# A four-layer recurrent model on one core: two products of each feed-forward row made ahead, in the score banks of the causal attention

## The chip, the core and the metric

The kernel runs on one core of one Trainium2 chip. The metric is the device time of the whole program in microseconds (us), as the median of several executions. PE is TensorE, DVE is VectorE, ACT is ScalarE, POOL is GpSimd and SP the engine that here only issues DMAs.

## The reference, cut to what matters

The model has a state of 2 x 1024 tokens of 128 channels. Each of four layers normalises the state, runs an attention over it and a feed-forward part, and adds their product to the state. All numbers are fp32. The change touches layers 2 and 3, whose attention is causal (16 heads of 8 channels); layer 2 turns queries and keys by rotary angles first, layer 3 has biases. Their feed-forward parts read the same normalised state x:

```
layer 2, 8 pairs of routed experts and one pair of shared ones, j = 0..8:
    y += W2[j] . ( gate(e, token) * silu(W1[j] . x) * (W3[j] . x) )      (no gate for j = 8)
layer 3, 16 experts, j = 0..15:
    a = min(Wg[j] . x + bg[j], 7),  b = clip(Wu[j] . x + bu[j], -7, 7)
    y += Wd[j] . ( gate(j, token) * a * sigmoid(1.702 a) * (b + 1) )
```

The gates come from a router: logits of x, a choice of experts by token, and weights that are zero for those not chosen. So every expert is computed for every token.

## The kernel before

`layer` (L3087) runs a layer: `attention_weights` and `ffn_weights` give tiles and pairs for their loads, then `rotary_attention` or `biased_attention` runs a prologue (normalise, queries, keys, values, split in bf16 parts that go through DRAM into "stacks"), then `causal_attention` (L2092), `project_out` (L2713) and the experts (`grouped_ffn`, L1185, in layer 2, `clamped_ffn`, L1289, in layer 3).

**The causal attention** has 8 units (two batches by four groups of four heads). Each unit needs two passes. The first finds the maximum of each row of scores: 20 "max" jobs on PE (L2393 to L2400) into one of two double banks (`room`), each reduced by one DVE instruction (L2276). After the 6th job (query half 0) and after the 20th (half 1) the maxima are negated and split in three bf16 parts on DVE, turned by one small matmul ("maxima", L2405), copied (L2301) and sent by two small DMAs into three more rows of the query stack (L2346). The second pass makes the scores again, transposed and with the maximum subtracted by those rows ("st", L2424, one of three score banks `st`), takes the exponential on ACT (L2365) and multiplies by the values ("pv", L2443). Steps of half 0 wait for the first maxima rows, those of half 1 for the second ones. When a half is done its context is copied by ACT (L2372), turned ("context", L2412) and divided on DVE.

The order of all this on PE, and with it on DVE, ACT and SP, is written by `work_order` (L2134), a small planner that runs when the program is built. It keeps a clock `now` of PE, a list of first-pass jobs and a list of second-pass events, each in its own order, estimates from fixed costs when the head of each list could start, and takes the earlier one. PE executes the result in order: a step that waits holds all behind it. SP's list of DMAs follows the same order, after the loads of the stacks of units 1 and 2 and of the feed-forward weights (L2336 to L2340). The last three jobs belong to the router (logits, and turning the gates), whose chain of small DVE instructions lies between them.

**The feed-forward parts** go over four chunks of 512 tokens and, in each, over the experts j; a pair (chunk, j) is a step, 36 in layer 2 and 64 in layer 3. PE makes two products of 128 x 128 by 128 x 512 per step (`up`) into banks `a` and `b`, three of each, two steps ahead, and then the step's third product into `y` (L1227, L1333). In layer 2 ACT takes silu of `a` (L1240), DVE multiplies it by `b` (`mid`, L1259) and by the gate (`hid`, L1264). In layer 3 ACT makes `below` from `a` (L1343) one step ahead of `acted` from `below` (L1357), so ACT's queue is below(n+1), acted(n); DVE makes `linear` from `b` (L1369), then `mid` (L1374) and `hid` (L1380). The gate of a step comes as a row spread over all partitions by DMA (`GateRows`, four tiles, a row is loaded when the tile's last reader is done).

Of the kernel before, what the change touches and what calls it, by code (L numbers as in the profile page):

```python
# [1034 lines left out]

class GateRows:
# [23 lines left out]
class GroupRouter(TailRouter):  # L1060
# [6 lines left out]
    def __init__(self, nc, k, ph, landed, tiles):  # L1067
        super().__init__(nc, k, ph, landed)
        self.wr, *self.wide = tiles
        E, G = self.E, 4  # L1070
# [57 lines left out]
class SoftmaxRouter(TailRouter):  # L1128
# [7 lines left out]
    def __init__(self, nc, k, ph, landed, tiles):  # L1136
# [4 lines left out]
        self.gate_room, self.up_bias = ph.sb("r_gate_room", [P, E]), ph.sb("r_up_bias", [P, E])  # L1141

    def pool(self, pool):

        self.nc.gpsimd.memset(self.top[:], self.SLOPE * self.LIMIT).then_inc(self.filled, 1)

# [7 lines left out]
    def vector(self, dve, n, src, job_free, count):  # L1154
# [3 lines left out]
        if n == self.LOGITS:  # L1158
# [3 lines left out]
            nc.vector.tensor_scalar(self.gate_room[:], self.bias[:, 0, :], -1.0, self.LIMIT, ALU.mult, ALU.add).then_inc(self.steps, 1)  # L1162
            nc.vector.tensor_scalar(self.up_bias[:], self.bias[:, 1, :], 1.0, None, ALU.add).then_inc(self.steps, 1)
            chain.n = 2
            dve.wait_ge(self.steps, 2)
# [14 lines left out]
def grouped_weights(nc, ph, w):  # L1180
    gate, wide = ph.sb("gate", [P, 16]), [ph.sb("wide_" + name, [P, w["w_" + name].shape[1], P]) for name in ("gate", "up", "down")]
    return (gate, *wide), [(gate[:], w["gate"])] + [(tile[:], w["w_" + name]) for tile, name in zip(wide, ("gate", "up", "down"))]


def grouped_ffn(nc, k, w, tiles, r):  # L1185
# [3 lines left out]
    N, M, AHEAD = NCH * J, J - 1, 2  # L1189
    with phase(nc, "f2") as ph:  # L1190
# [5 lines left out]
        with nc.Block() as block:  # L1196

            @block.sync
            def _(sp):
                for m in range(NCH * M):  # L1200
                    c, j = divmod(m, M)
                    c0, j0 = divmod(m - rows.KEPT, M)
                    srcs = [r.dram[e:e + 1, c * CHUNK:(c + 1) * CHUNK] for e in (2 * j, 2 * j + 1)]
                    rows.load(sp, m, srcs, hid_ready, c0 * J + j0 + 1)

            @block.tensor
            def _(pe):
                def up(n):
                    c, j = divmod(n, J)
                    x = k.xnT[:, c * CHUNK:(c + 1) * CHUNK]  # L1210
                    if n >= 3:
                        pe.wait_ge(act_ready, n - 2)
                    nc.tensor.matmul(a[n % 3][:], w1T[:, j, :], x, start=True, stop=True).then_inc(a_done, 1)
                    if n >= 3:
                        pe.wait_ge(mid_ready, n - 2)
                    nc.tensor.matmul(b[n % 3][:], w3T[:, j, :], x, start=True, stop=True).then_inc(b_done, 1)

                for n in range(AHEAD):
                    up(n)
                for n in range(N):  # L1220
                    c, j = divmod(n, J)
# [160 lines left out]

H = 16
# [1784 lines left out]
```

## Time and profile before

| | us |
|---|---|
| median of 3 runs (lowest, highest) | 1840.69 (1837.62, 1852.1) |
| the profiled execution, its own time | 1835.92 |
| its span in the trace | 1834.1 |
| PE busy, share of the span | 1523.2, 83% |
| DVE busy | 1168.7, 64% |
| ACT busy | 914.5, 50% |
| POOL busy | 473.3, 26% |
| layer 2: first matmul of the attention to last product of the experts | 932.0 to 1308 |
| layer 3: the same | 1351.4 to 1822.5 |

A busy time is the sum of an engine's instructions. Matmuls are pipelined, so a busy PE need not be at its peak. The granted clock (PEclk) is the mean share of TensorE's full clock of 2.4 GHz; it has two levels, 1.00 and 0.50 (1.2 GHz). In a timeline a bracket behind a group holds the idle time of its engine before it and what ended it.

### The profile page before, as it was taken

Reading aid. Unit: us, or ns where it says so; the run is one execution under the profiler, and the core shown is the slowest. Engines: PE = TensorE matmul, PEld = TensorE weight load, DVE = VectorE, ACT = ScalarE, POOL = GpSimd, SP = SyncE. Lnnn points to the kernel's source line nnn. Section 1 sums busy time; section 2 is a strip of 40 time slices with the busy share of each in tenths; the row PEclk is TensorE's granted clock in tenths of the full one; section 3 lists DMA queues with packets and bytes.
Section 4 is the critical chain, followed back from the end, with each engine's and each line's share of the span. In section 5 each row is a group of like instructions: output and inputs, shape, how many; then the busy total and the mean of one; then the engine's idle time right before and its main releaser. Section 6 shows DMA issues by size and latency. Waiting matters only on the chain. (4 is left out here: it accounts for less than half of the span.)

```text
span 1834.1 us, 32772 instructions
## 1 busy us (share of the span) xinstructions
PE 1523.2 (83%) x12067; PEld 733.9 (40%) x12067; DVE 1168.7 (64%) x2509; ACT 914.5 (50%) x1755; POOL 473.3 (26%) x408
## 2 busy tenths in 40 slices
PE   5989744998888888988748988889848988889998
PEld 4656422434433433334313434344323343344443
DVE  4323667745855855834668988635658988617777
ACT  1332232666656666665225666642224666555453
POOL 0701437756756756730210000000020000000000
PEclk9989865999999999999768999899868999789999
DMA  7232257666766666730240100022170010004332
GB/s 216 84 94 73 58 164 185 181 160 172 179 160 164 178 169 168 183 84 1 75 148 20 37 20 20 2 73 90 33 225 20 20 37 20 2 6 111 100 98 80
DMA packets 218198, 179.13 MB, mean 98 GB/s; under 512 B 57600, under 2 KB 186136, under 8 KB 217624
## 3 DMA queue, kind: packets, MB, share of 16 engines
q1 hardware_dynamic: 207928, 160.34, 32.4%
q10 hardware_dynamic: 8064, 12.51, 2.4%
q0 software_dynamic: 2048, 4.20, 0.8%
q8 instruction: 96, 1.57, 0.4%
q14 instruction: 62, 0.51, 0.1%
HBM read 108.64 MB, written 67.64 MB: 96 GB/s over the span
## 5 line engine op out<-in xcount | busy, mean ns | idle before, releaser
L1924 DVE TENSOR_REDUCE a1a_partial<-a1a_room 128x4 f32<-128x1024 f32 x192 | 226.4, 1221 | 30.8 <-PE a1a_room L1989 30.2
L2365 ACT ACTIVATE a3a_probsT<-a3a_st 128x512 f32<-128x512 f32 (+2 forms) x320 | 155.7, 560 | 123.5 <-PE a3a_st L2431 73.6
L1883 ACT ACTIVATE a1a_probsT<-a1a_st 128x512 f32<-128x512 f32 (+1 forms) x416 | 204.7, 575 | 13.9 <-PE a1a_st L2022 12.6
L2365 ACT ACTIVATE a2a_probsT<-a2a_st 128x512 f32<-128x512 f32 (+2 forms) x320 | 155.6, 560 | 111.1 <-PE a2a_st L2431 65.8
L2276 DVE TENSOR_REDUCE a3a_maxima<-a3a_room 128x2 f32<-128x1024 f32 (+3 forms) x160 | 170.2, 1113 | 34.5 <-PE a3a_room L2400 23.7
L2276 DVE TENSOR_REDUCE a2a_maxima<-a2a_room 128x2 f32<-128x1024 f32 (+3 forms) x160 | 170.2, 1113 | 25.6 <-PE a2a_room L2400 19.2
L1788 POOL TENSOR_TENSOR a1a_shifted<-a1a_shifted,a1a_best 128x1024 f32<-128x1024 f32 x64 | 121.7, 1903 | 93.5 <-DVE a1a_best L1930 67.2
L1920 DVE CUSTOM_DVE_ANT_0 a1a_shifted<-a1a_room,a1a_bands 128x256 f32<-128x256 f32 x256 | 93.3, 421 | 75.4 <-PE a1a_room L1989 67.4
L2059 PE MATMUL a1a_ctx<-a1a_probsT,a1a_vpad 128*9 128x512 f32 (+3 forms) x1408 | 139.3, 494 | 0.8
L1989 PE MATMUL a1a_room<-stack 48*128 48x128 bf16 (+1 forms) x1376 | 108.2, 261 | 37.1 <-DVE a1a_partial L1924 19.0
L2022 PE MATMUL a1a_st<-stack 51*128 51x512 bf16 (+3 forms) x576 | 116.7, 317 | 19.7 <-ACT a1a_nearT L1890 6.2
L1886 ACT ACTIVATE a1a_probsT<-a1a_st 128x512 f32<-128x512 f32 x128 | 73.3, 603 | 111.9 <-PE a1a_st L2031 111.9
L2325 POOL COPY a_vpad<-a_values 128x256 f32<-128x256 f32 x16 | 6.3, 400 | 423.9 <-PE a3a_ctx L2443 210.9
L2424 PE MATMUL a3a_st<-stack 51*128 51x512 bf16 (+3 forms) x384 | 87.5, 353 | 16.5 <-ACT a3a_probsT L2365 8.2
L2443 PE MATMUL a3a_ctx<-a3a_probsT,a_vpad 128*32 128x512 f32 (+3 forms) x768 | 90.0, 547 | 7.8 <-ACT a3a_probsT L2365 4.7
L2424 PE MATMUL a2a_st<-stack 51*128 51x512 bf16 (+3 forms) x384 | 84.7, 342 | 13.1 <-ACT a2a_probsT L2365 9.1
L1989 PEld LDWEIGHTS a1a_room<-stack 48*128 48x128 bf16 x1376 | 46.4, 99 | 117.7 <-DVE a1a_partial L1924 62.1
L2443 PE MATMUL a2a_ctx<-a2a_probsT,a_vpad 128*32 128x512 f32 (+3 forms) x768 | 86.4, 526 | 4.6 <-ACT a2a_ctxT L2372 2.0
L2393 PE MATMUL a2a_room<-stack 48*128 48x512 bf16 (+3 forms) x384 | 67.0, 351 | 25.5 <-PEq L2511 15.9
L1343 ACT ACTIVATE f_below<-f_a,r_r_gate_room 128x512 f32<-128x512 f32 x64 | 44.0, 687 | 85.7 <-PE f_a L1317 85.6
L2393 PE MATMUL a3a_room<-stack 48*128 48x512 bf16 (+3 forms) x384 | 66.9, 350 | 23.6 <-DMA stack<-k 14.0
L1800 POOL TENSOR_TENSOR a1a_beyond<-a1a_probsT,c_beyond_mask 128x512 f32<-128x512 f32 x56 | 70.9, 1271 | 55.1 <-ACT a1a_probsT L1886 55.1
(464 smaller groups left out, 3092.1 us busy)
## 6 DMA issues: line engine op xcount, KB each, us to landing
a1a_bands<-a_band SPq DMA_DIRECT2D x112, 192.0 KB, 3.8
a_near<-a1a_shifted SPq DMA_DIRECT2D x112, 192.0 KB, 3.1
a1a_near<-a_near SPq DMA_DIRECT2D x64, 256.0 KB, 4.0
f_rows<-l_gates SPq DMA_DIRECT2D x64, 256.0 KB, 3.0
a_band<-a1a_r_mix SPq DMA_DIRECT2D x64, 254.0 KB, 3.5
stack<-q SPq DMA_DIRECT2D x96, 96.0 KB
f_rows<-l_gates SPq DMA_DIRECT2D x64, 128.0 KB, 3.0
stack<-k SPq DMA_DIRECT2D x32, 96.0 KB
```

Of the source, the lines that this page charges most:

```text
L1788: nc.gpsimd.tensor_tensor(shifted[:, V % 2, t], shifted[:, V % 2, t], best[:, V % 2, :, t:t + 1].broadcast_to([P, HG, NEAR]), ALU.subtract ...
L1883: nc.scalar.activation(dst, src, ACT.Exp).then_inc(exp_done, 1)
L1920: ins = nc.vector.tensor_tensor_reduce(shifted[:, V % 2, t, place, :], src[:, place // 2, place % 2, :], band[i][:, place, :], 1.0, LOWEST ...
L1924: nc.vector.tensor_reduce(partial[:, g % 2, :, 1 + r].rearrange("p (a s) -> p a s", a=2), src, X_AXIS, ALU.max).then_inc(job_free, 1)
L1989: mm = nc.tensor.matmul(dst[:, lo + i * P:lo + (i + count) * P], q, rows_of(sides[edge], place, STACK)[:, c * P:(c + count) * P], start=Tr ...
L2022: mm = nc.tensor.matmul(dst[:, to:to + count * P], rows_of(sides[edge], place + j, ALL_ROWS)[:, c * P:(c + 1) * P], query_rows(q_stack, pl ...
L2059: mm = nc.tensor.matmul(ctx[32 * h:32 * h + DH + 1, lo * P:hi * P], vpad[b][right][:, c, h, :], probsT[:, block_index(V, at) % BLOCK_ROOMS ...
L2276: nc.vector.tensor_reduce(best, scores, X_AXIS, ALU.max).then_inc(job_free, 1)
L2365: nc.scalar.activation(probsT[:, block_at % BLOCK_ROOMS, place:place + heads, lo:], src, ACT.Exp).then_inc(exp_done, 1)
L2393: mm = nc.tensor.matmul(dst[:, end - width:end], query_rows(q_stack, place, STACK, I // HALF_TILES)[:, I % HALF_TILES * P:(I % HALF_TILES ...
L2424: mm = nc.tensor.matmul(dst[:, j * width:(j + 1) * width], rows_of(k_stack, place + j, ALL_ROWS)[:, c * P:(c + 1) * P], query_rows(q_stack ...
L2443: mm = nc.tensor.matmul(ctx[32 * PAIRED[h]:32 * PAIRED[h] + 32, lo:], vpad[b][:, c, PAIRED[h], :], probsT[:, block_at % BLOCK_ROOMS, h, lo ...
```

## The change

Of every chunk, the products of experts 0 and 1 (four products, 16 per layer) are made by PE inside `causal_attention`, as events "first" ahead of all second-pass events. Each goes through a score bank; ACT copies it to an SBUF tile (in layer 3 `below` and the biased `b` are made at once). Six of the 16 tiles lie in tensors that are idle then (two in `gT`, four in `xn_one`), ten are new. The planner takes a first product when its estimate is earlier than that of the next max job, from 4.0 us on. In the feed-forward part, the steps of experts 0 and 1 are moved between the others (`steps_of_chunks`), `up` skips them, and ACT and DVE read the tiles. The weights of these experts are loaded first, before the stacks of units 1 and 2; the rest is loaded where all was. In layer 3 the two bias tiles are made by POOL at the start instead of by DVE in the router's chain, and POOL's part of the router comes after unit 1's values instead of unit 3's.

```diff
+class FirstProducts:
+    EACH, TILES = 2, 10
+    COUNT = 2 * NCH * EACH
+    def __init__(self, nc, k, ph, landed, left, right):
+        self.nc, self.k, self.landed, self.weights = nc, k, landed, (left, right)
+        own, free = ph.sb("first", [P, self.TILES, CHUNK]), k.xn_one[:].rearrange("p t d -> p (t d)")
+        self.tiles = [k.gT[:, (NCH - 1 - i) * CHUNK:(NCH - i) * CHUNK] for i in range(2)]
+        self.tiles += [free[:, i * CHUNK:(i + 1) * CHUNK] for i in range(4)] + [own[:, i, :] for i in range(self.TILES)]
+    def place(self, c, j, side):
+        return self.tiles[(c * self.EACH + j) * 2 + side]
+    def tensor(self, pe, i, dst):
+        step, side = divmod(i, 2)
+        c, j = divmod(step, self.EACH)
+        if i == 0:
+            pe.wait_ge(*self.landed)
+        return self.nc.tensor.matmul(dst[:], self.weights[side][:, j, :], self.k.xnT[:, c * CHUNK:(c + 1) * CHUNK], start=True, stop=True)
+    def scalar(self, act, i, src):
+        return self.nc.scalar.copy(self.tiles[i], src[:])
+class ClampedProducts(FirstProducts):
...
+        if side == 0:
+            return self.nc.scalar.activation(self.tiles[i], src[:], ACT.Relu, bias=self.room[:, j:j + 1], scale=-1.0)
+        return self.nc.scalar.activation(self.tiles[i], src[:], ACT.Identity, bias=self.bias[:, j:j + 1])
+def steps_of_chunks(J, places):
+    later = [j for j in range(FirstProducts.EACH, J)]
+    for j, at in enumerate(places):
+        later.insert(at, j)
+    return [(c, j) for c in range(NCH) for j in later]
...
 def grouped_ffn(nc, k, w, tiles, r):
+    N, AHEAD, first = NCH * J, 2, r.first
+    seq = steps_of_chunks(J, (2, 6))
+    made = [n for n in range(N) if seq[n][1] >= first.EACH]
...
+                issued = 0
                 for n in range(N):
-                    if n + AHEAD < N:
-                        up(n + AHEAD)
+                    while issued < min(len(made), sum(m <= n for m in made) + AHEAD):
+                        up(issued)
+                        issued += 1
...
+                    if j < first.EACH:
+                        src = first.place(c, j, 0)
+                    else:
+                        q = made.index(n)
+                        act.wait_ge(a_done, q + 1)
+                        src = a[q % 3][:]
+                    nc.scalar.activation(acted[:, n % 3, :], src, ACT.Silu).then_inc(act_ready, 1)
...
 def clamped_ffn(nc, k, w, tiles, r):
+    seq = steps_of_chunks(E, (4, 12))
...
+                    if j < first.EACH:
+                        nc.vector.tensor_scalar(linear[:, n % 2, :], first.place(c, j, 1), LIMIT + 1.0, None, ALU.min).then_inc(linear_ready, 1)
...
 def causal_attention(...)
+    FIRST = router.first.COUNT
     def work_order():
+        events = [("first", 0, i) for i in range(FIRST)] + [(what, U, n) for U in range(UNITS) for what, n in second_pass]
...
+                if what == "first":
+                    event_at = max(exps[-ST_BANKS] + latency, first_landed)
...
+                if what == "first":
+                    now += 870
+                    exps.append(max(exps[-1], now + latency) + 700)
...
-                    if U == UNITS // 2 - 1:
+                    if U == 1:
                         router.pool(pool)
             def _(sp):
+                start_loads(sp, *after[0])
                 for U in range(1, len(stack)):
                     sp.wait_ge(stored[U % BATCH], 16 * (len(queries.stored) + len(keys.stored)))
                     load_unit(U)
-                for pairs, sem in after:
-                    start_loads(sp, pairs, sem)
+                start_loads(sp, *after[1])
...
             def _(act):
+                    if what == "first":
+                        act.wait_ge(st_done, n + 1)
+                        router.first.scalar(act, n, st[n % ST_BANKS]).then_inc(exp_done, 1)
...
             def _(pe):
+                    if what == "first":
+                        if n >= ST_BANKS:
+                            pe.wait_ge(exp_done, n - ST_BANKS + 1)
+                        router.first.tensor(pe, n, st[n % ST_BANKS]).then_inc(st_done, 1)
```

## Rows read from the trace of the kernel before

**Rows 1.** Windows: busy us of each engine in 50 us stretches, then clock and DMA.
```profile
1000.00:1050.00 50.00, 46.67 (x582) 20.81 (x578) 44.94 (x64) 34.02 (x71) 0.55 (x2) 1.00 0.06 18
...
1250.00:1300.00 50.00, 50.00 (x118) 22.11 (x117) 25.46 (x37) 12.63 (x22) 0.00 (x0) 1.00 0.26 87
...
1700.00:1750.00 50.00, 50.00 (x117) 21.77 (x116) 37.49 (x56) 25.61 (x40) 0.00 (x0) 1.00 0.32 97
```
**Rows 2.** Windows at the start of the two attentions (PE, PEld, DVE, ACT, POOL, PEclk).
```profile
932.00:950.00 18.00, 9.49 (x85) 4.22 (x87) 14.38 (x18) 1.28 (x1) 0.74 (x2) 0.50 0.65 202
...
967.00:990.00 23.00, 21.92 (x216) 8.60 (x218) 18.75 (x28) 14.31 (x29) 0.00 (x0) 0.82 0.01 2
...
1351.00:1373.00 22.00, 9.12 (x83) 3.98 (x83) 14.38 (x18) 0.18 (x1) 0.74 (x2) 0.50 0.72 226
```
**Rows 3.** Timeline: first score step on PE, reduces and last maxima on DVE.
```profile
949.64 0.62 PE L2424 MATMUL a2a_st<-stack 51*128 51x512 bf16 x2 [3.22 <-DMA stack<-a2a_parts]
...
951.35 2.27 DVE L2276 TENSOR_REDUCE a2a_maxima<-a2a_room 128x2 f32<-128x1024 f32 x2 [3.34 <-PE a2a_room L2393]
...
960.57 0.18 DVE L2282 TENSOR_TENSOR a2a_maxima<-a2a_maxima 128x16 f32<-128x16 f32 x1
...
1373.36 0.61 PE L2424 MATMUL a3a_st<-stack 51*128 51x512 bf16 x2 [7.55 <-DMA stack<-a3a_parts]
...
1375.08 2.27 DVE L2276 TENSOR_REDUCE a3a_maxima<-a3a_room 128x2 f32<-128x1024 f32 x2 [7.67 <-PE a3a_room L2393]
...
1384.12 0.18 DVE L2282 TENSOR_TENSOR a3a_maxima<-a3a_maxima 128x16 f32<-128x16 f32 x1
```
**Rows 4.** Timeline of ACT at the start of the attentions of layers 2 and 3.
```profile
932.00 1.28 ACT L2365 ACT_TABLE_LOAD   x1 [3.40 <-PEq L2511]
950.38 2.83 ACT L2365 ACTIVATE a2a_probsT<-a2a_st 128x512 f32<-128x512 f32 x6 [17.10 <-PE a2a_st L2431]
...
968.04 2.21 ACT L2365 ACTIVATE a2a_probsT<-a2a_st 128x512 f32<-128x512 f32 x4 [9.19 <-PE a2a_st L2424]
...
1374.11 2.83 ACT L2365 ACTIVATE a3a_probsT<-a3a_st 128x512 f32<-128x512 f32 x6 [22.92 <-PE a3a_st L2431]
```
**Rows 5.** Groups by form: busy us, mean ns of one, idle before it.
```profile
L1213 PE MATMUL f_a<-xnT,l_wide_gate 128*128 128x512 f32 x72 | 36.9, 593 | 1.0 <-PEq L2719 1.0
...
L1369 DVE TENSOR_SCALAR f_linear<-f_b,r_r_up_bias 128x512 f32<-128x512 f32 x64 | 47.7, 745 | 2.3 <-PE f_b L1320 2.3
```
**Rows 6.** Timeline of a steady step of layer 3's experts.
```profile
1702.25 1.02 PE L1317 MATMUL f_a<-xnT,l_w_up 128*128 128x512 f32 x2
...
1703.11 1.02 PE L1320 MATMUL f_b<-xnT,l_w_up 128*128 128x512 f32 x2
...
1703.31 0.69 ACT L1343 ACTIVATE f_below<-f_a,r_r_gate_room 128x512 f32<-128x512 f32 x1 [0.79 <-PE f_a L1317]
...
1705.42 0.69 DVE L1380 SCALAR_TENSOR_TENSOR f_hid<-f_mid,f_rows 128x512 f32<-128x512 f32 x1
...
1706.54 1.02 PE L1333 MATMUL f_y<-f_hid,l_w_down 128*128 128x512 f32 x2
```
**Rows 7.** Timeline of PE at the end of layer 3's experts.
```profile
1817.19 1.02 PE L1333 MATMUL f_y<-f_hid,l_w_down 128*128 128x512 f32 x2
1819.39 1.12 PE L1333 MATMUL f_y<-f_hid,l_w_down 128*128 128x512 f32 x2 [1.18 <-DVE f_hid L1380]
1821.50 2.01 PE L1333 MATMUL f_y<-f_hid,l_w_down 128*128 128x512 f32 x2 [0.99 <-DVE f_hid L1380]
```
**Rows 8.** Groups by form, DVE: the normalisation of layer 3's prologue.
```profile
L2665 DVE TENSOR_SCALAR xn_one<-x,a3j_moments,a3j_rstd 128x128 f32<-128x128 f32 x16 | 4.3, 344 | 0.1
```
**Rows 9.** Windows of 5 us: start of layer 2's attention, end of layer 3's.
```profile
950.00:955.00 5.00, 5.00 (x44) 1.92 (x42) 2.20 (x3) 2.83 (x6) 0.00 (x0) 0.54 0.00 0
955.00:960.00 5.00, 4.43 (x74) 2.39 (x70) 5.00 (x5) 2.61 (x6) 0.00 (x0) 1.00 0.01 3
...
1595.00:1600.00 5.00, 4.74 (x27) 1.36 (x29) 0.00 (x0) 3.08 (x7) 0.00 (x0) 0.50 0.00 0
```

More of the change, by code:

```diff
@@ L1141, in __init__ @@
         self.gate_room, self.up_bias = ph.sb("r_gate_room", [P, E]), ph.sb("r_up_bias", [P, E])
+        self.first = ClampedProducts(nc, k, ph, early, tiles, self.gate_room, self.up_bias)
     def pool(self, pool):
         self.nc.gpsimd.memset(self.top[:], self.SLOPE * self.LIMIT).then_inc(self.filled, 1)
+        pool.wait_ge(*self.first.landed)
+        self.nc.gpsimd.tensor_scalar(self.gate_room[:], self.bias[:, 0, :], -1.0, self.LIMIT, ALU.mult, ALU.add).then_inc(self.first.ready, 1)
+        self.nc.gpsimd.tensor_scalar(self.up_bias[:], self.bias[:, 1, :], 1.0, None, ALU.add).then_inc(self.first.ready, 1)
     def tensor(self, pe, n, dst, job_free, first):
@@ L1199, in _ @@
             def _(sp):
-                for m in range(NCH * M):
-                    c, j = divmod(m, M)
-                    c0, j0 = divmod(m - rows.KEPT, M)
+                for m, n in enumerate(gated):
+                    c, j = seq[n]
                     srcs = [r.dram[e:e + 1, c * CHUNK:(c + 1) * CHUNK] for e in (2 * j, 2 * j + 1)]
-                    rows.load(sp, m, srcs, hid_ready, c0 * J + j0 + 1)
+                    rows.load(sp, m, srcs, hid_ready, gated[m - rows.KEPT] + 1)
             @block.tensor
@@ L1218, in _ @@
-                for n in range(AHEAD):
-                    up(n)
-                for n in range(N):
-                    c, j = divmod(n, J)
-                    if n + AHEAD < N:
-                        up(n + AHEAD)
-                    if j == 0 and c >= 2:
+                    if q >= 3:
+                        pe.wait_ge(act_ready, made[q - 3] + 1)
+                    nc.tensor.matmul(a[q % 3][:], w1T[:, j, :], x, start=True, stop=True).then_inc(a_done, 1)
+                    if q >= 3:
+                        pe.wait_ge(mid_ready, made[q - 3] + 1)
@@ L1350, in _ @@
                 for n in range(N):
-                    c, j = divmod(n, E)
+                    c, j = seq[n]
                     if n + 1 < N:
                         room_below(n + 1)
-                    act.wait_ge(below_ready, n + 1)
                     if n >= 3:
                         act.wait_ge(mid_ready, n - 2)
-                    nc.scalar.activation(acted[:, n % 3, :], below[:, n % 2, :], ACT.Silu, bias=r.top[:, 0:1], scale=-SLOPE).then_inc(act_ready, 1)
-                    if c and j == AHEAD:
+                    if j < first.EACH:
+                        src = first.place(c, j, 0)
+                    else:
+                        q = made.index(n)
+                        act.wait_ge(below_ready, q + 1)
+                        src = below[:, q % 2, :]
+                    nc.scalar.activation(acted[:, n % 3, :], src, ACT.Silu, bias=r.top[:, 0:1], scale=-SLOPE).then_inc(act_ready, 1)
+                    if c and n % E == AHEAD:
                         gates_of(c - 1)
@@ L2228, in causal_attention @@
     for event in order:
+        if event[0] == "first":
+            act_order.append(event)
         if event[0] == "st":
```

146 lines of the change are left out of this document (81 added, 65 removed).

## The prediction

> **What bounds the kernel now.** I read the windows first. In the two feed-forward stages PE is busy 50.00 of 50 us at granted clock 1.00 while DVE has 25.46 and 37.49 [rows 1]: both stages are PE's. In the middle of the attention PE is at 46.67 of 50, so there is little room there either; but in the first 18 us of the attention of layer 2 it is busy 9.49 us, in the first 22 us of layer 3 it is 9.12, both at clock 0.50 [rows 2]. The timeline says why: PE stands at the first score step of the second pass and waits for the maxima rows to come back by DMA, 3.22 us in layer 2 and 7.55 us in layer 3, and as its queue is in order DVE then gets no room to reduce, 3.34 and 7.67 us [rows 3]. ACT has nothing to do before the first exponential, 17.10 and 22.92 us [rows 4]. So the change takes PE work out of stages that PE fills and puts it where PE, ACT and the three score banks lie idle.
>
> **What the feed-forward stages lose.** A product is two matmul records of 593 ns that overlap; from the start of one to the next it is 1702.25 to 1703.11, 0.86 us [rows 5, 6]. Sixteen products per layer are 13.7 us of PE.
>
> Layer 2: a step is three products, 2.58 us, and DVE needs about half of that [rows 1]. Its hid is ready more than a step before PE wants it, so a step with one product instead of three doesn't starve PE. The steps that lose their products lie four or five apart, so the gate rows, loaded four steps ahead, get about 1.72 us less of some ten. Gain 13.7 us, all of it.
>
> Layer 3 is closer. In a steady step `a` of the next step starts at 1702.25, its below on ACT at 1703.31, hid of this step at 1705.42 for 0.69, and its y at 1706.54 [rows 6]: hid ends 3.86 us after its neighbour's `a` began, 0.43 us before PE uses it. DVE alone needs 2.11 us per step: that is the distance of the last two y of the stage, 1819.39 and 1821.50, where no product stands between [rows 7]. Take up(e-1), the products issued three steps ahead of an early step e, at time 0. PE then has y(e-3), up(e+1), y(e-2), up(e+2), y(e-1) and reaches y(e) at nine products, 7.73 us. DVE ends hid(e-2) at 3.86; from there it isn't held by ACT, for acted(e-1) no longer stands behind a below that waits for PE; two steps of 2.11 bring hid(e) to 8.08. PE waits 0.35 us and saves 1.72: 1.37 us net, 8 times, 10.9 us. The f_linear of an early step reads SBUF instead of PSUM. The trace has 745 ns for the PSUM form of 512 columns and 344 ns for a tensor_scalar on 128 columns in SBUF [rows 5, 8]. I take 745 (same line, same length); with 344 DVE is 0.40 us sooner and PE doesn't wait at all, 13.7 us.
>
> The Trainium skill bears on this one term: VectorE: DVE Perf Modes, in "The perf-mode tier table" and "Why PSUM operands drop a tier", gives a tensor_scalar on fp32 in SBUF two elements per cycle and one with a PSUM operand. By that rule the early f_linear would take an estimated 0.4 us, the wait would vanish and layer 3 would give 13.7 us instead of 10.9; no row here shows such an instruction at 512 columns.
>
> **What the attention gets.** I worked the order through with the planner's own numbers. The first product comes after the 4th max job, the rest singly or in pairs between the following ones, the 16th just ahead of the 19th; the first score step follows that job. Before, it followed the 13th. PE's train from the 4th job is 16 products (13.7 us at full clock) and 15 max jobs. The 13 jobs before the first score step took 9.49 us at half clock [rows 2], 0.73 each, so about 0.37 at full: 5.5 us. With PE busy without a break from the fourth microsecond on I expect the clock to rise about 5 us later, as it did after 949.64: 0.54 in 950 to 955, 1.00 in the next window [rows 9]. Those 5 us do half their work, so 2.5 us more: 21.7 us. The train ends some 25.4 us after the first matmul (932.0 and 1351.4), at 957.4 and 1376.8. The first score step comes 7.8 us later in layer 2 and 3.4 in layer 3.
>
> That isn't the time the attention loses, since the second half of the unit waits for rows of its own: ACT idles 9.19 us before 968.04 [rows 4], as those rows need the 20th reduce, which ends at 960.57 and 1384.12 [rows 3]. After the change DVE is no longer stopped by the score step; it idles only where a product or two stand before its room. Its last two reduces follow the train, about 3 us: 960.4 and 1379.8. So the gate of the second half stays in layer 2 and comes 4.3 us earlier in layer 3, and the delayed first half runs in the gap that was idle. The clock should gain too: behind that gap its mean was 0.82 over 967 to 990 [rows 2], which is 8.3 us at the lower level and 4.1 us of PE work; without the gap it stays up. Of the 4.1 I take 2, since ACT and DVE hold PE for part of that time. Against this stand new frictions, which I take at 1 us in layer 3, none in layer 2 where the gap covers them. Sum: -2 us in layer 2, -5 in layer 3. Bounds: the whole delay of the first score step passed on, +7.8 and +3.4; all of clock and gate gained, -4 and -8.4.
>
> **Edits taken at nothing.** The 16 evacuations on ACT, about 0.69 us each like a below [rows 6], 11 us, lie in ACT's 17.10 and 22.92 us; without that cover they would hold the score banks. The load of the exponentials' table, 1.28 us at 932.00 [rows 4], moves behind the last evacuation: 0 to 1.28 per layer, taken as 0, because the first half has slack. SP issues the two early loads before its wait for the stored stacks, so they are in front of the bulk; the later weights go out where they did, less a tenth of their bytes. The maxima rows behind them stay late, but PE is no longer waiting there. The first product waits for the early loads; behind it in PE's queue stands the 5th max job, and DVE waits for that: 0 to 2 us a layer, the nearest row being the 3.22 us that PE waited for rows behind the bulk [rows 3]; I take 0, as the loads have 4 us. GpSimd's vpad copies of units 0 and 1 come before its new wait, the next one is due a unit later. The two bias operations leave DVE's router chain and go to GpSimd: 0 to -0.4 us. Loads of stacks still follow score steps; their counts are only offset.
>
> **Sum.** -13.7 - 10.9 - 2 - 5 = -31.6 us. The profiled execution took 1835.92 us (span 1834.1), so 1804.3 by its own account. The median shown is 1840.69, 4.8 above it; I give the forecast on the median's footing: 1809.
>
> **Rivals.**
> (a) The start of the second pass sets the end after all: units follow each other with little idle PE, so 7.8 and 3.4 us are passed on and nothing comes back from gate or clock. -24.6 + 11.2 = -13.4: 1827. For it: PE 46.67 of 50 in the middle [rows 1]. Against it: the 9.19 us before 968.04 [rows 4], which a start 7.8 us late doesn't lengthen.
> (b) Slower: the clock doesn't rise during the train. Max jobs are short and products wait for banks, and PE has been seen busy 4.74 of 5 us at 0.50 [rows 9]. Then all 16 products cost 1.72 us and the jobs 0.73: 38.5 us instead of 21.7, the first score step comes 24.6 and 20.2 us late, the 20th reduce with it, and little of it is hidden: +44.8 - 24.6 = +20, 1861. It decides from the point where a layer's delay exceeds 12.3 us, that is when some 9 of 16 products run at the lower level.
> (c) Layer 3's early steps don't get the head start on ACT that I count on. The last steps of the stage, where two y stand without a product between, are 2.20 us apart (1817.19 to 1819.39) [rows 7], only 0.38 less than a step. Then layer 3 gives 3 us and the sum is -24: 1817.
> The clock in the last 60 us of each attention, at 0.50 for long stretches [rows 9], may shift either way by several us with the new timing; it widens every case by about 8 us.
>
> **How the numbers follow.** Forecast 0.58, (a) 0.22, (b) 0.08, (c) 0.12. One per cent, 18.4 us, is about what a measurement of this kernel can tell from no change. Faster by more: nearly all of the forecast (0.55), 0.8 of (c), a tenth of (a): 0.67. Slower: most of (b): 0.07. The rest 0.26. The range leaves out (b) and the far ends of the spread: 1795 (the forecast with all bounds of layer 3 and the attention gained) to 1832 ((a) and half its spread).
>
> **What would show it.** In the profile after: the feed-forward windows still at PE 50.00 and the two stages 13 to 14 and 10 to 14 us shorter; 8 waits of PE for f_hid in layer 3 of 0.3 to 0.4 us, or none; sixteen matmuls with evacuations before the first exponential; clock 1.00 from about the eighth microsecond of each attention; the second gap of ACT down from 9.19 to a few us; the 20th reduce 4 us nearer to the start in layer 3. I am wrong if the attention of layer 2 grows by more than 5 us, or if the clock stays at 0.50 through the train.

## The result and the profile after

| | us |
|---|---|
| before, median beside the change (4 runs) | 1844.57 |
| after, median (lowest, highest) | 1818.78 (1813.65, 1823.78) |
| ratio after/before, 95% interval | 0.9854 (0.9824, 0.9885) |
| the profiled execution, before and after | 1835.92 and 1819.34 |
| its span, before and after | 1834.1 and 1817.5 |

The change is faster by 1.5%. Timed again later beside 11 runs of the kernel before, it gave 0.9814 (0.9775, 0.9853). By stages the two profiled executions differ like this; a second profile of each kernel (experiments e0 and e8) stands behind the first.

| stage, us | before | after | forecast |
|---|---|---|---|
| attention of layer 2, first matmul to the first one of its projection | 276.2, 276.3 | 285.5, 282.8 | -2 |
| experts of layer 2, first product to the start of the last y | 92.4 | 78.7 | -13.7 |
| attention of layer 3, as in layer 2 | 290.6, 293.7 | 290.2, 289.3 | -5 |
| experts of layer 3, as in layer 2 | 172.4, 172.4 | 160.6, 160.6 | -10.9 |

PE's first product and last y of the experts show the two gains, layer 2 before and after, then layer 3 before and after (the last y of layer 3 before is in [rows 7], at 1821.50):

```profile
1215.31 1.10 PE L1213 MATMUL f_a<-xnT,l_wide_gate 128*128 128x512 f32 x2 [1.05 <-PEq L2719]
1305.51 2.74 PE L1227 MATMUL f_y<-f_hid,l_wide_down 128*128 128x512 f32 x6
...
1225.79 1.10 PE L1272 MATMUL f_a<-xnT,l_wide_gate 128*128 128x512 f32 x2 [1.05 <-PEq L2814]
1301.51 3.60 PE L1286 MATMUL f_y<-f_hid,l_wide_down 128*128 128x512 f32 x8
...
1649.11 1.10 PE L1317 MATMUL f_a<-xnT,l_w_up 128*128 128x512 f32 x2 [1.05 <-PEq L2719]
...
1645.53 1.10 PE L1390 MATMUL f_a<-xnT,l_w_up 128*128 128x512 f32 x2 [1.05 <-PEq L2814]
1806.12 1.13 PE L1406 MATMUL f_y<-f_hid,l_w_down 128*128 128x512 f32 x2 [0.99 <-DVE f_hid L1464]
```

So the feed-forward stages gave 25.5 us together, where 24.6 was forecast, and the attention of layer 2, which was to get shorter, took 9.3 back in the first profile and 6.5 in the second.

The windows of the kernel after, over the first 50 us of layer 2's attention, answer to [rows 2, 9] (busy us of PE, PEld, DVE, ACT and POOL, then clock, DMA share, GB/s):

```profile
933.20:938.20 5.00, 3.10 (x37) 2.05 (x38) 3.65 (x4) 0.00 (x0) 0.88 (x3) 0.50 0.60 163
938.20:943.20 5.00, 5.00 (x18) 1.66 (x17) 2.45 (x3) 1.17 (x2) 0.00 (x0) 0.66 0.69 189
943.20:948.20 5.00, 5.00 (x18) 1.64 (x19) 3.24 (x7) 2.34 (x4) 0.00 (x0) 1.00 0.88 219
...
963.20:968.20 5.00, 4.30 (x46) 1.92 (x48) 2.67 (x8) 2.69 (x6) 0.00 (x0) 0.73 0.00 0
968.20:973.20 5.00, 4.76 (x74) 2.88 (x70) 4.32 (x6) 2.62 (x6) 0.00 (x0) 0.93 0.01 2
973.20:978.20 5.00, 4.22 (x27) 0.92 (x24) 3.71 (x7) 3.54 (x7) 0.00 (x0) 0.75 0.01 3
978.20:983.20 5.00, 4.82 (x49) 2.22 (x49) 3.49 (x6) 2.78 (x6) 0.00 (x0) 0.90 0.01 2
```

The clock rises to 1.00 by the tenth microsecond, as hoped, and PE is busy without a break through the train (the 16 products and the max jobs between them). But behind the train, from 963 on, it is below 1.00 again in four windows, where I had counted on it to stay up.

The timeline of PE (start, length, line, operation) shows the train's beginning, its rhythm and its end, against [rows 3]:

```profile
937.88 2.08 PE L1056 MATMUL a2a_st<-xnT,l_wide_gate 128*128 128x512 f32 x2 [1.23 <-DMA l_wide_up<-in_L_ffn_w_up]
...
948.73 1.13 PE L1056 MATMUL a2a_st<-xnT,l_wide_up 128*128 128x512 f32 x2
949.79 0.39 PE L2484 MATMUL a2a_room<-stack 48*128 48x512 bf16 x2
950.11 1.12 PE L1056 MATMUL a2a_st<-xnT,l_wide_gate 128*128 128x512 f32 x2
...
961.37 0.38 PE L2519 MATMUL a2a_st<-stack 51*128 51x512 bf16 x2
...
963.71 0.39 PE L2519 MATMUL a2a_st<-stack 51*128 51x512 bf16 x1 [1.32 <-ACT a2a_probsT L2456]
```

PE waits 1.23 us for the early weights. At full clock a product takes 1.06 us (948.73 to 949.79) between max jobs, where in the feed-forward stage it takes 0.86, and with its max job a pair takes 1.38; I had 0.86 + 0.37. The first score step (961.37) comes 28.2 us after the first matmul (933.2), where I had 25.4. Then PE stops for 1.32 us: for ACT. Its timeline says why, against [rows 4]:

```profile
940.00 0.58 ACT L1059 COPY gT<-a2a_st 128x512 f32<-128x512 f32 x1 [10.22 <-PE a2a_st L1056]
...
961.16 0.58 ACT L1059 COPY r_first<-a2a_st 128x512 f32<-128x512 f32 x1 [0.79 <-PE a2a_st L1056]
961.76 1.28 ACT L2456 ACT_TABLE_LOAD   x1
963.06 2.83 ACT L2456 ACTIVATE a2a_probsT<-a2a_st 128x512 f32<-128x512 f32 x6
968.51 1.85 ACT L2456 ACTIVATE a2a_probsT<-a2a_st 128x384 f32<-128x384 f32 x4 [2.62 <-PE a2a_st L2526]
971.22 0.85 ACT L2456 ACTIVATE a2a_probsT<-a2a_st 128x256 f32<-128x256 f32 x2 [0.86 <-PE a2a_st L2526]
973.50 2.06 ACT L2456 ACTIVATE a2a_probsT<-a2a_st 128x512 f32<-128x512 f32 x4 [1.44 <-PE a2a_st L2519]
```

The exponentials' table is loaded between the last evacuation and the first exponential. The 9.19 us of idle ACT before the second half have become 1.44, as forecast; yet the second half itself starts 40.3 us after the first matmul (973.50 less 933.2) and not 36.0 as before (968.04 less 932.04, [rows 4]). Of these 4.3 us, 2.2 come with the 20th reduce, which ends 30.76 us after the first matmul where it was 28.53, and 2.1 behind it.

In layer 3's experts the timeline of PE and DVE around an early step, and the groups of the line that makes its `linear` (lowest, median and highest ns; first and last start), answer to [rows 6, 7]:

```profile
1672.72 1.02 PE L1390 MATMUL f_a<-xnT,l_w_up 128*128 128x512 f32 x2
...
1678.61 0.42 DVE L1449 TENSOR_SCALAR f_linear<-xn_one 128x512 f32<-128x512 f32 x1
...
1679.59 2.08 PE L1406 MATMUL f_y<-f_hid,l_w_down 128*128 128x512 f32 x4
1679.79 0.69 DVE L1464 SCALAR_TENSOR_TENSOR f_hid<-f_mid,f_rows 128x512 f32<-128x512 f32 x1
...
1681.50 1.02 PE L1390 MATMUL f_a<-xnT,l_w_up 128*128 128x512 f32 x2
```

```profile
L1449 DVE TENSOR_SCALAR f_linear<-r_first x5: 418/419/421, 1718.4 to 1797.2; 128x512 f32<-128x512 f32 x5
L1449 DVE TENSOR_SCALAR f_linear<-xn_one x2: 420/420/420, 1678.6 to 1698.9; 128x512 f32<-128x512 f32 x2
L1449 DVE TENSOR_SCALAR f_linear<-gT x1: 418/418/418, 1659.5 to 1659.5; 128x512 f32<-128x512 f32 x1
```

The early `linear` takes 0.42 us, not the 0.745 that I took. The two y of the early step and its neighbour take 1.91 us (1679.59 to 1681.50) where two products take 1.72.

### The profile page after: what moved, and what is told of

The parts are those of the page before. It is cut to its first block and busy times, and to the rows that moved or that the text cites. A ratio compares the mean times of both kernels' runs of the same rounds, so it can differ in the third digit from the quotient of the medians.

```text
span 1817.5 us, 32776 instructions
## 1 busy us (share of the span) xinstructions
PE 1530.6 (84%) x12067; PEld 731.7 (40%) x12067; DVE 1165.3 (64%) x2507; ACT 928.5 (51%) x1779; POOL 473.4 (26%) x410
## 5 line engine op out<-in xcount | busy, mean ns | idle before, releaser
L1862 POOL TENSOR_TENSOR a1a_r_mix<-a1a_r_raw,a1a_r_mix 128x512 f32<-128x512 f32 x64 | 81.3, 1270 | 5.0
L2484 PE MATMUL a2a_room<-stack 48*128 48x512 bf16 (+3 forms) x384 | 64.4, 339 | 19.0 <-PEq L2606 15.9
L1418 ACT ACTIVATE f_below<-f_a,r_r_gate_room 128x512 f32<-128x512 f32 x56 | 38.5, 687 | 79.4 <-PE f_a L1390 79.3
```

The costliest lines, as they stand in the source:

```text
L1862: nc.gpsimd.tensor_tensor(mix[:], raw[:], mix[:], ALU.subtract).then_inc(mixed, 1)
```

## The experiments

In the readings below "the last max job" is the start of the last first-pass job after the first matmul of that attention, and "the tail" is the time from there to the first matmul of the projection. They were 220.0 and 56.2 us before, 225.5 and 60.0 after in layer 2; 224.2 and 66.4, 223.5 and 66.7 in layer 3. "Length" is the whole attention, as in the table above. Expectations that speak of the change mean the kernel after.

### e0: the kernel before, a second profile

No edit.

> The kernel before, unchanged, for a second profile. In its first profile the attention of layer 2 took 276.2 us, of which the last 56.2 come after its last max job; with the change 285.5 and 60.0. Theory: the 5.5 us up to the last max job are the price of the train and come back in every profile; the 3.8 us after it are TensorE's clock, which stood at 0.50 for different stretches. Then this profile shows the last max job again at 220 +-1 us after the start, but a tail that differs from 56.2 by 2 us or more. Rival: the tail is fixed by the kernel too: 56.2 +-1.

Measured: 1840.25 us. Layer 2: last max job 220.1, tail 56.1. Layer 3: last max job 227.3 (224.2 in the first profile), tail 66.4. My theory fell: layer 2's tail came back within 0.1 us, so the kernel before shows no such spread there. The spread in this pair was in layer 3, 3.1 us, and the first profile of before had drawn the shorter time.

### e2: the change without its products

```diff
-    FIRST = router.first.COUNT
+    FIRST = 0
...
                         router.pool(pool)
+                        for tile in router.first.tiles:
+                            nc.gpsimd.memset(tile, 0.5)
```

> The kernel after without the 16 early products of a layer and their evacuations; the feed-forward steps read tiles filled with 0.5, so this leaves out a part of the computation. The early loads, the bias tiles on GpSimd and the changed feed-forward stages stay. Theory: the whole growth of the attention of layer 2 is the train: its last max job returns from 225.5 to 220 +-1 us after the start and its length from 285.5 to 276 to 280, in layer 3 the last max job is at 224 +-1; the feed-forward stages stay 14 and 12 us shorter than before; about 1812 us. Rival: the moved loads or GpSimd's earlier part hold the attention up: the last max job of layer 2 stays at 223 or later.

One execution, with a part of the computation left out. Measured: 1813.52 us; layer 2: last max job 220.3, length 276.4; layer 3: 223.9 and 290.2; experts as with the change (160.6 in layer 3). So all that the attention of layer 2 grew by comes from the products, their evacuations and what these push back. The loads that were moved forward and GpSimd's earlier part cost nothing, as I had taken it.

### e3: one expert ahead, 8 products per layer

```diff
-    EACH, TILES = 2, 10
+    EACH, TILES = 1, 2
...
-    seq = steps_of_chunks(J, (2, 6))
+    seq = steps_of_chunks(J, (4,))
...
-    seq = steps_of_chunks(E, (4, 12))
+    seq = steps_of_chunks(E, (8,))
```

> The kernel after with one expert ahead instead of two: 8 early products per layer, at place 4 of the chunk in layer 2 and 8 in layer 3. Theory: the first products lie in PE's idle time and the later ones are paid at about 1.06 us each where the feed-forward stage saves 0.86: the last max job of layer 2 comes at 221 +-1.5 us (before 220.0, with 16 products 225.5), the feed-forward stages are 6.9 and about 6.2 us shorter than before, and the time is 4 to 8 us above that of the change, near 1825. Rival: the price of the train is one of starting it (clock, loads, the late first score step), the same for 8 products as for 16: last max job at 224 or later and about 1832 us.

Measured: 1825.02 us, ratio 0.9896 (0.9862, 0.9930). Layer 2: last max job 220.0, length 276.1; layer 3: 224.5 and 290.8; its experts 166.3, 6.1 less than before. Eight products are free, as the theory had it. ACT's timeline shows what they leave as it was:

```profile
949.52 0.58 ACT L1059 COPY r_first<-a2a_st 128x512 f32<-128x512 f32 x1 [1.08 <-PE a2a_st L1056]
950.12 1.28 ACT L2456 ACT_TABLE_LOAD   x1
951.97 2.83 ACT L2456 ACTIVATE a2a_probsT<-a2a_st 128x512 f32<-128x512 f32 x6 [0.57 <-PE a2a_st L2526]
...
968.87 1.72 ACT L2456 ACTIVATE a2a_probsT<-a2a_st 128x512 f32<-128x512 f32 x3 [9.42 <-PE a2a_st L2519]
```

The table load is followed by 0.57 us of waiting for PE, so it is covered here, and the gap before the second half is still 9.42 us. In the order that the planner writes, everything but the products stands as before with 8 of them, the first score step behind the 13th max job; with 16 that step stands behind the 19th. The gap closes only with the second eight. With them layer 2's attention grows by 6.5 to 9.3 us and its experts save 6.8 more. That does not yet make the products themselves the price: with 16 the table load is no longer covered either, and the next experiment parts the two.

### e1, e7, e9: the table loaded ahead of the evacuations

```diff
             def _(act):
+                nc.scalar.activation(warm[:], k.ident[:, 0:1], ACT.Exp)
                 for what, U, n in act_order:
```

One kernel, three times: one execution (e1), then several (e7), then several on one chip with the change (e9 beside e8, which has no edit).

> The kernel after with one exponential of a single column put ahead of ACT's evacuations, so that the exponentials' table is loaded in ACT's idle time. Theory: the table load of 1.28 us, which I had costed at nothing, stands between the last evacuation and the first exponential, and PE's queue waits for it: the first exponential comes 28.5 instead of 29.8 us after the start of the attention of layer 2 (29.2 instead of 30.5 in layer 3), the first reload of a stack 60.0 and 58.0 instead of 61.1 and 59.1, some 2 us in all. Rival: the first half of the unit has slack and the marks after the first exponential stay within 0.4 us.

> The kernel after with the exponentials' table loaded ahead of the evacuations, the same as before, now timed. Theory: the 1.28 us of the table load made PE idle behind the train, and the lower clock that followed cost more than the load itself: 5 to 9 us below the change's 1818.8, 1810 to 1814. Rival: the single time of 1811.66 was a lucky clock in the last part of layer 3's attention (60.1 instead of 66.7 us): 1815 to 1818, and that part back at 66.

> The kernel after, unchanged, on the same chip and beside the same runs as the two below. Theory: 24 to 28 us below the kernel before; the attention of layer 2 again at 225.5 +-0.5 us for its last max job with the clock under 1.00 behind the train, since that part came alike in every profile of one program; the part after the last max job anywhere between 56 and 62 us.

> The kernel after with the exponentials' table loaded ahead of the evacuations, beside the change on one chip. Theory: the start of both attentions gains 3.5 to 5 us in layer 2 and 0.5 to 3.5 in layer 3, as read from the last max job of two profiles, so the median is 4 to 8 us below the change. Rival: the granted clock of the last part gives it back: within 2 us of the change.

| layer 2 | first exponential | last max job | tail | length |
|---|---|---|---|---|
| the change, two profiles | 29.8, 30.2 | 225.5, 226.7 | 60.0, 56.2 | 285.5, 282.8 |
| table ahead, three profiles | 28.9, 29.0, 28.7 | 222.0, 220.6, 220.3 | 59.1, 61.8, 61.8 | 281.1, 282.4, 282.1 |

ACT's timeline of e1 in layer 2 shows the load at the front and the first exponential right behind the last copy:

```profile
935.05 1.28 ACT L2445 ACT_TABLE_LOAD   x1 [3.40 <-PEq L2607]
...
963.26 0.59 ACT L1059 COPY r_first<-a2a_st 128x512 f32<-128x512 f32 x1 [0.79 <-PE a2a_st L1056]
963.95 2.83 ACT L2457 ACTIVATE a2a_probsT<-a2a_st 128x512 f32<-128x512 f32 x6
```

The first exponential is 1.2 us earlier on the mean, but the last max job is 3.5 to 6.4 us earlier. With the table ahead all 16 products stand where they stood, and the last max job comes only 0.3 to 2.0 us later than in the kernel before (220.0): up to there the price was the load and what followed it, not the products, and the rival's slack in the first half wasn't there. The loss arises early: the 25th of the first unit's 40 exponentials starts 50.2 and 53.0 us after the first matmul in the change and 46.9, 47.0 and 46.7 with the table ahead.

Windows of e1 and of e8 over the 20 us behind the train show the difference. First the table ahead:

```profile
965.10:970.10 5.00, 4.54 (x73) 2.72 (x73) 4.24 (x10) 3.44 (x8) 0.00 (x0) 1.00 0.00 0
970.10:975.10 5.00, 4.65 (x58) 1.81 (x50) 4.86 (x9) 2.63 (x7) 0.00 (x0) 1.00 0.01 2
975.10:980.10 5.00, 4.24 (x40) 1.43 (x39) 3.75 (x7) 3.67 (x8) 0.00 (x0) 1.00 0.02 5
980.10:985.10 5.00, 4.82 (x48) 1.89 (x44) 4.92 (x5) 3.32 (x8) 0.00 (x0) 1.00 0.01 1
```

and the change in its second profile:

```profile
963.00:968.00 5.00, 4.02 (x44) 1.85 (x46) 2.73 (x8) 2.96 (x7) 0.00 (x0) 0.76 0.00 0
968.00:973.00 5.00, 5.00 (x48) 2.89 (x48) 3.01 (x4) 2.10 (x5) 0.00 (x0) 0.50 0.01 2
973.00:978.00 5.00, 4.89 (x44) 1.70 (x40) 3.66 (x7) 2.46 (x6) 0.00 (x0) 0.71 0.00 0
978.00:983.00 5.00, 4.33 (x32) 1.83 (x31) 2.50 (x5) 2.45 (x6) 0.00 (x0) 0.66 0.02 3
```

In each of the four windows PE is busy for 4 to 5 us in both, but its clock is 1.00 in the one and 0.66 on the mean in the other. A mean of 0.66 is 13.7 of 20 us at the lower level, in which a PE that is busy throughout does 6.8 us less; by the clock of the change's first profile (0.73, 0.93, 0.75, 0.90) it is 3.4 us. The loss at the 25th exponential is close to that, 6.0 to 6.4 us in the second profile and 3.2 to 3.6 in the first. So in layer 2 the load of 1.28 us opened a pause of 1.3 us in PE, the clock went down behind it, and that cost several times the pause. That the pause is what brought the clock down rests on two profiles against three.

In layer 3 the same load (first exponential at 30.5 and 29.6 us) left the clock at 1.00 behind it in both profiles of the change, up to 60 us after the first matmul; its last max job is at 223.5 and 222.6 us there, and at 223.0, 219.9 and 220.0 with the table ahead.

Yet the whole isn't faster. e7 had 1812.37 us, inside the 1810 to 1814 that its theory gave, but beside a kernel before at 1839.72, so its ratio, 0.9851 (0.9820, 0.9881), is that of the change. e9 had 1816.65, 0.9848 (0.9810, 0.9886), beside 1812.18 of the change on the same chip, where 4 to 8 us less than the change was expected: that theory fell. For the change itself (e8) the theory had given 24 to 28 us below the kernel before and a last max job at 225.5 +-0.5; it was 36 us below (1848.26) and at 226.7. What the start gains in layer 2, the tail gives back on that chip (61.8 against 56.2, so 282.1 against 282.8 in all), and executions of one program lie up to 17 us apart (e7: 1803.92 to 1821.24), more than what is left. That the table load is paid in the first unit of layer 2 is shown; that moving it makes the kernel faster by itself isn't.

### e4, e5: the early weights loaded in the prologue

```diff
                 start_loads(sp, loads[plan.first:], rest_landed)
+                if early is not None:
+                    start_loads(sp, *early)
...
-                start_loads(sp, *after[0])
                 for U in range(1, len(stack)):
...
-        latency, rows_in_dma, load_time, switch, first_landed = 250.0, 4500.0, 9000.0, 100.0, 4000.0
+        latency, rows_in_dma, load_time, switch, first_landed = 250.0, 4500.0, 9000.0, 100.0, 0.0
```

e5 has the line of e1 as well.

> The kernel after with the early weights loaded at the start of the prologue and the planner free to place a product from time 0 instead of 4.0 us; the table load stays where it is. Theory: PE's wait of 1.23 us for the weights is gone and the train begins some 3 us sooner, so the first exponential comes at 26 to 28 us instead of 29.8; but the table load still opens an idle stretch of PE behind the train and the clock falls there again: granted clock below 0.95 somewhere in the 20 us after the first score step, last max job of layer 2 at 223 or later. Rival: the late loads were the cause of the late train and all that follows: clock 1.00 there, last max job at 222 or earlier.

> The loads of the early weights in the prologue, the planner free from time 0, and the exponentials' table loaded ahead of the evacuations. Theory: both delays of the start go; first exponential of layer 2 at 25 to 27 us (28.9 with the table alone), last max job at 220 to 221.5, about 2 us below the kernel with the table alone, near 1810. Rival: PE is full there in any case, and what starts earlier only waits longer: last max job at 222 as with the table alone, and no difference in time.

Measured, e4: 1824.98 us; the first exponential of layer 2 at 27.1, but the clock again at 0.50 to 0.95 in five windows behind the train, and the last max job at 225.5 as with the change. So in this one execution starting the train 3 us sooner brought nothing while the table load stood behind it. e5: 1815.35, 0.9876 (0.9855, 0.9897); first exponential at 25.9, last max job at 222.7 and 222.8 in the two layers, which is no better than the table alone. Its clock, too, fell behind the train of layer 2, to 0.97 and 0.69 in two windows (969.4 to 979.4), with no load there, so a load isn't the only thing that can go ahead of such a fall. The rival was right here: the 1.23 us that PE waits for weights, which I had costed at nothing, do cost nothing.

### e6, e10: six products at the end of the prologue

The prologue's PE is idle for 15.9 us before the first max job in layer 2 and 13.7 in layer 3. Six products, whose tiles lie in `gT` and `xn_one`, go there; ten stay behind the first max jobs. e10 is the same kernel, beside e8 and e9.

```diff
+                if ahead is not None:
+                    pe.wait_ge(*ahead.landed)
+                    pe.wait_ge(prod_ready, 4)
+                    for i in range(ahead.N):
+                        if i == 4:
+                            pe.wait_ge(written[plan.jobs[J - 2][3]], seen(plan.jobs[J - 2][3], BATCH - 1, J - 2, 1))
+                        ahead.tensor(pe, i, places[i]).then_inc(ahead.made, 1)
...
+                if ahead is not None:
+                    ahead.evacuate(act, 0, places)
...
+                if ahead is not None:
+                    ahead.evacuate(dve, 1, places)
```

> As the kernel with both, but the first 6 of the 16 products of a layer are made at the end of the prologue, where PE is idle for 15.9 us in layer 2 and 13.7 in layer 3 while the last parts are stored; four go to banks that are free by then, two to banks whose last reader is done, ACT and DVE evacuate three each behind their last parts. Theory: products in idle time are free: the prologue stays as long as it was within 0.6 us, the first exponential of layer 2 comes at 20 to 22 us, the last max job at 220 +-1, the length of that attention at 276 to 279; 3 to 5 us below the kernel with the table alone. Rival: the evacuations or the changed clock hold the last stores and the first max job comes over 1 us later, which eats the gain.

> The kernel with 6 products at the end of the prologue, beside the change on one chip. Theory: its attention of layer 2 is as long as before the change, 276 +-1, against 285.5; in layer 3 nothing is gained but the clock's luck; the median is 7 to 11 us below the change. Rival: half of that or less, because the last part of the attention takes it back.

The timeline of PE in e10, where `a2j` is the prologue of layer 2:

```profile
917.17 1.95 PE L2697 MATMUL a2j_bank<-l_wide,xnT 128*128 128x128 f32 x16
918.96 1.02 PE L1058 MATMUL a2j_mix<-xnT,l_wide_gate 128*128 128x512 f32 x2
...
925.91 1.02 PE L1058 MATMUL a2j_bank<-xnT,l_wide_up 128*128 128x512 f32 x2
934.99 0.40 PE L2518 MATMUL a2a_room<-stack 48*128 48x128 bf16 x4 [8.06 <-PEq L2641]
```

The six are done 8 us before PE is wanted. The prologue is as long as it was: 54.4 us in e6 from its first matmul to the first max job, 54.0 with the change. Layer 2: first exponential 19.1 and 19.3, last max job 220.0 and 220.2, length 276.1 and 276.3, the same as before the change with all 16 products made. Layer 3: last max job 223.2 and 223.7, nothing gained. Times: e6 1811.64, 0.9850 (0.9827, 0.9874), beside 1812.37 with the table alone (e7); e10 1813.28, 0.9816 (0.9775, 0.9857), the change beside it 0.9814. The theory of the stage is right; the 3 to 5 and the 7 to 11 us of the whole were not to be seen.

### e11: the better start of each layer

Layer 2 from e6, and for layer 3 all 16 products behind the first max jobs with the table ahead of them (0 in the prologue, the planner free from 4.0 us).

> The best start of each layer put together: in layer 2 six products at the end of the prologue and ten behind the first max jobs; in layer 3 all sixteen behind the first max jobs with the exponentials' table loaded ahead of them. Theory: layer 2's attention 276 +-1 us, layer 3's last max job at 220 to 223 us, the feed-forward stages as with the change; 8 to 12 us below the change by the profile's stages, which is a ratio to the kernel before of 0.976 to 0.980. Rival: as with the two versions before it, what the stages show is lost in the spread from execution to execution, and the ratio lies at 0.981 to 0.986 like that of the change.

Measured: 1805.04 us (1800.62 to 1810.12), ratio 0.9781 (0.9751, 0.9810). Layer 2: last max job 220.1, length 276.3. Layer 3: last max job 219.9, length 286.7. Its interval lies below that of the change's first timing (0.9824 to 0.9885), and overlaps that of the second (0.9775 to 0.9853). That is the ratio that its theory gave, and the lowest here; it was not run beside the change on one chip.

## Why the prediction was right, and where it was wrong

The time fell into the forecast range: 1809 us in 1795 to 1832, and medians of 1818.78 and 1812.18 were measured, 25.8 and 36.1 us below the kernel before. The sum was made for the profiled execution, and there it was -31.6 and measured -16.6 (span 1834.1 to 1817.5; -24.1 in the second pair, 1838.4 to 1814.3), because the two attentions, forecast at -7, took 8.9. The profiled execution of before was one of its faster ones (1835.92, where medians of 1839.72 to 1848.26 were measured beside the experiments), so part of the agreement is luck.

**Layer 2's experts, -13.7: right.** Their last y starts at 1307.7 before and 1304.5 after, behind first products at 1215.31 and 1225.79: 92.4 and 78.7 us. Between them PE waited for no engine in either.

**Layer 3's experts, -10.9: right, the size a little off, -11.8.** The term that was mis-sized is the early `linear`: 745 ns taken, 419 measured. The Trainium skill's rule (VectorE: DVE Perf Modes, "The perf-mode tier table") gave an estimated 0.4 us for it; with 418 to 421 ns the trace agrees. Put into my own working, `hid` of the early step should come 8.08 - 0.33 = 7.75 us after its `a`; the rows above show it ending at 1680.48, 7.76 after 1672.72, and PE was due there at 7.73. So the wait of 0.35 us was not there. But the 13.7 us that I had tied to that weren't either: seven of the eight early steps still lose 0.19 or 0.20 us (1.91 for two y in a row instead of 1.72) and one 0.55, together the 1.9 us that separate 11.8 from 13.7. Why the second y starts late by these 0.1 to 0.2 us isn't shown.

**Layer 2's attention, -2: wrong, +9.3 and +6.5.** Two steps of the sum failed. The first is "the load of the exponentials' table ... taken as 0, because the first half has slack". With eight products it has (e3); with sixteen the slack is gone, and the price was not 0 to 1.28 us but 3.5 to 6.4 at the last max job (the change's two profiles against e1, e7 and e9), the load and PE's lower clock behind it together. So what the prediction said of the clock, "without the gap it stays up", failed with it. The Trainium skill (ScalarE: Activation LUTs, "What ACT_TABLE_LOAD costs") gives 1283 ns for the load and 1380 more for a drain; the trace shows 1.28 and no drain beside it, as the exponential starts 0.02 us behind the load, and the trace decides here.

The second is the length of the train: 28.2 us in layer 2 and 28.7 in layer 3 to the first score step where I had 25.4. A product costs 1.06 us between max jobs and not 0.86, with its max job 1.38 and not 1.23, fifteen times 0.15, and 0.5 at the start. With that the 20th reduce ended 30.8 us after the first matmul in layer 2 and 31.3 in layer 3, where I had 28.4 in both; the gate of the second half, which was to stay, moved with it. This second error cost little: with the table ahead the train is as long (20th reduce at 30.8 to 31.1 in layer 2) and the second half starts 38.1 to 38.4 us after the first matmul, yet the last max job is within 0.3 to 2.0 us of the kernel before. The rest of the growth, 3.8 us in the first profile and none in the second, is the tail; for its clock the prediction had left the sum alone and widened the range by about 8 us.

**Layer 3's attention, -5: -0.4, and -4.4 in the second pair, where the kernel before had drawn 3.1 us more.** So the sign is hardly shown and the size is off. The step that failed is the gate again: it has the same late train, and the 20th reduce came 1.4 us sooner than before (31.3, 32.7) and not 4.3. The load taken at nothing stands in this term too: with the table ahead the length was 286.7 and 286.8 us in e7 and e9, 3.9 below the shorter profile of before.

**The sign of being wrong** that I had set, layer 2's attention longer by more than 5 us, was there. Rival (a), in which the start of the second pass is passed on to the end, gave +7.8 and +3.4 us: in layer 2 its size is nearer to what happened than my forecast, in layer 3 the two pairs lie between both. Its mechanism is not what happened: with the table ahead the first score step is as late (28.2 to 28.5 us where it was 17.6), and the last max job isn't. Rival (b), the clock staying at 0.50 in the train, did not happen: 1.00 from the tenth microsecond. Rival (c) didn't either.

**What stays open.** The tail of layer 2 was 56.1 or 56.2 us in all seven profiles with no more than ten products behind the first max jobs, and 59.1 to 61.8 in six of the seven with sixteen; e8 alone had 56.2. The change itself gave both 60.0 and 56.2, so instructions and their order do not decide it; what differs is the clock. Windows from the last max job to the projection show it for the change, e8 and e9:

```profile
1158.70:1218.67 59.97, 51.34 (x404) 20.42 (x404) 25.79 (x148) 34.27 (x72) 0.00 (x0) 0.80 0.02 3
...
1159.66:1215.81 56.15, 46.79 (x405) 19.65 (x404) 25.74 (x148) 34.41 (x72) 0.00 (x0) 0.88 0.02 4
...
1154.20:1216.00 61.80, 53.60 (x405) 20.88 (x404) 25.80 (x148) 34.40 (x72) 0.00 (x0) 0.75 0.02 3
```

DVE and ACT are busy alike in all three, PE is not. By the mean clock of the window, the time at 0.50 is 13.7 us in all eight short tails, 20.5 in the two of 59.1, 23.9 in the two of 60.0 and 31.0 in the two of 61.8. No run tells what makes the clock come back in the one and not in the other.

## What to carry to other kernels

Work moved into an idle stretch is free while it fits there; beyond that, ask what it pushes back. Here 8 products in layer 2's stretch were free, and so were ten with six more in the 15.9 us in which PE waits for a prologue to be stored. With all sixteen in the one stretch the attention grew by 6.5 to 9.3 us, about what the experts save by the second eight. But the products were not the larger part of that price. A table load had stood hidden in ACT's idle time; behind the new work it held PE for 1.3 us, and in layer 2, where the clock went down behind it, 3.5 to 6.4 us were lost at the last max job. So when an engine gets new work ahead of its old, ask what stood hidden in the idle time before. And a stage that is shown shorter need not show in the time of the whole: the kernels that took these us out of the start were not measurably faster than the change, except perhaps the last.

## What the runs showed of the hardware

- In layer 2 a pause of 1.3 us in a PE that had been busy at 1.00 for 20 us was followed by 20 us of windows at 0.50 to 0.93, in both profiles; without it, in the same order of work, the clock was 1.00 over that stretch in three. In layer 3 the same pause left it at 1.00: such a pause can go ahead of a fall of the clock, it needn't. In e5 the clock fell to 0.69 in one window without a load there.
- Sixteen copies (layer 2) and sixteen Relu or Identity with a bias (layer 3) needed no table of their own: in e1 they follow the exponentials' table and no other load stands before the exponentials, and in the change they run before that table is loaded.
- A product in fp32 took PE 1.06 us between jobs in bf16 of another shape, 0.86 in a row of its own kind (948.73 to 949.79; [rows 6]), both at clock 1.00.
- A `tensor_scalar` in fp32 on 128x512 took DVE 418 to 421 ns with its source in SBUF and 743 to 750 ns with its source in PSUM.
- One stage of one program can differ by several us through the clock alone: layer 3's tail was 60.1, 66.8 and 66.8 us in three profiles of the kernel with the table ahead, with 17.1, 41.0 and 41.0 us of it at 0.50.
